# One core, cross attention and quantised FFN: the first stage's statistics, activation table and weight sums in another order

## The reference

```python
def _layernorm(x, axis=-1, eps=1e-05):
    m = jnp.mean(x, axis=axis, keepdims=True)
    v = jnp.var(x, axis=axis, keepdims=True)
    return (x - m) / jnp.sqrt(v + eps)

x = x + _L0_xattn_ref(_layernorm(x), ctx_768, Wq, bq, Wk, bk, Wv, bv, Wo, bo)
x = x + _L0_ffn_ref(_layernorm(x), W1, b1, W2, b2)          # weights to -1, 0, 1
x = x + _L1_xattn_ref(ctx_768, _layernorm(x), mask, ...)     # ctx_768 is normalised in it
x = x + _L1_ffn_ref(_layernorm(x), ...)                      # 8 experts, two for each token

# in _L0_xattn_ref
q = x @ Wq + bq; k = y @ Wk + bk; v = y @ Wv + bv
out = softmax(q k^T * scale) v;  return out @ Wo + bo
# in bitlinear of _L0_ffn_ref
w_scale = clip(mean(abs(W)), EPS)
Wq = clip(round(W / w_scale), -1, 1) * w_scale
```

## Time and profile before

| what | us |
|---|---|
| median of three executions | 954.39 |
| lowest, highest of them | 952.44, 960.53 |
| the profiled execution's own time | 951.19 |
| its span in the trace | 949.4 |
| PE busy in the span | 878.0 |
| DVE busy | 638.1 |
| ACT busy | 531.1 |
| POOL busy | 384.7 |

### The profile page before, as it was taken

The page is one execution under the profiler, slowest core; times in us unless marked ns, Lnnn a source line. Parts: engine busy times, 40 slices in busy tenths (PEclk is TensorE's granted clock), DMA queues, the critical chain, the costliest instruction groups (busy, mean ns, idle before and its releaser), DMA issues.

```text
span 949.4 us, 15088 instructions
## 1 busy us (share of the span) xinstructions
PE 878.0 (92%) x4301; PEld 612.3 (64%) x4302; DVE 638.1 (67%) x1282; ACT 531.1 (56%) x847; POOL 384.7 (41%) x319
## 2 busy tenths in 40 slices
PE   8987769889999999999999999999999999999991
PEld 4644445545555555555457887778888887888881
DVE  4899987765567467456388778846666666566666
ACT  2548875546665755765555434326666665666650
POOL 2134424526667647657505545502222222222210
PEclk9999999999999999999999999999999999999996
DMA  9400000008487587578565200078711298426305
GB/s 308 102 1 1 0 0 1 1 4 319 160 319 281 195 332 293 200 302 312 214 248 189 100 1 1 12 274 364 277 60 33 69 353 337 182 78 259 108 24 177
DMA packets 49908, 154.05 MB, mean 162 GB/s; under 512 B 6266, under 2 KB 24438, under 8 KB 44236
## 3 DMA queue, kind: packets, MB, share of 16 engines
q1 hardware_dynamic: 46124, 144.25, 40.3%
q0 software_dynamic: 3744, 9.31, 3.1%
HBM read 97.85 MB, written 56.62 MB: 163 GB/s over the span
## 4 chain that ended last, share of the span: by engine, by line
PE 63%; DVE 16%; DMA 6%; ACT 6%; issue 5%; POOL 2%; SPq 1%; DVEq 0%; ACTq 0%; POOLq 0%
PE banks L1032 12%; PE banks L1283 6%; PE banks L1285 6%; PE banks L1284 6%; DMA aux<-moe_x,small 4%; PE banks L1001 4%; PE banks L1024 3%; PE banks L1025 3%; PE banks L939 2%; PE banks L1320 1%; PE banks L1322 1%; PE banks L1321 1%; PE banks L988 1%; PE banks L1296 1%; PE banks L1046 1%
## 5 line engine op out<-in xcount | busy, mean ns | idle before, releaser
L1032 PE MATMUL banks<-wexp 128*65 128x512 f32 (+1 forms) x288 | 149.2, 599 | 2.8 <-ACT wexp L1590 2.8
L662 POOL TENSOR_TENSOR cv_hl<-wexp,cv_hl 128x1024 fp32r<-128x1024 f32 x45 | 108.5, 2418 | 53.7 <-ACT cv_hl L1567 53.1
L1283 PE MATMUL banks<-ring,x_hi 128*128 x312 | 127.4, 408 | 0.0
L1285 PE MATMUL banks<-ring,x_lo 128*128 x312 | 122.1, 391 | 0.0
L1284 PE MATMUL banks<-ring,x_hi 128*128 x312 | 122.1, 391 | 0.0
L1590 ACT ACTIVATE wexp<-banks 128x512 f32<-128x512 f32 x128 | 76.3, 598 | 75.3 <-PE banks L1025 74.8
L2065 DVE TENSOR_REDUCE small<-banks 128x1 bf16<-128x1101 f32 x64 | 83.6, 1307 | 38.0 <-PE banks L1001 38.0
L1726 ACT ACTIVATE banks<-wexp 128x1024 f32 x72 | 73.4, 1020 | 47.7 <-DVE aux L2446 47.7
L1704 ACT ACTIVATE aux<-banks 128x512 f32<-128x512 f32 x78 | 46.6, 597 | 63.0 <-PE banks L1285 46.9
L1024 PE MATMUL banks<-q_hi,k_hl 128*128 128x512 f32 x144 | 75.3, 523 | 1.7 <-ACT q_lo L1558 1.0
L734 POOL DMA_INDIRECT moe_y<-aux,small x20 | 20.6, 1030 | 115.8 <-DVE aux L2456 115.8
(11 more groups left out here) (365 smaller groups left out, 2188.9 us busy)
## 6 DMA issues: line engine op xcount, KB each, us to landing
wsplit<-cv_hl SPq DMA_DIRECT2D x45, 1024.0 KB, 7.9
ring<-wsplit SPq DMA_DIRECT2D x32, 1280.0 KB
wexp<-in_L_ffn_w SPq DMA_DIRECT2D x40, 512.0 KB, 5.8
wexp<-in_expert_biases SPq DMA_DIRECT2D x8, 1152.0 KB, 6.6
ring<-wsplit SPq DMA_DIRECT2D x4, 1024.0 KB, 8.7
wexp<-moe_y SPq DMA_DIRECT2D x7, 512.0 KB, 6.1
wexp<-in_L_ffn_sw SPq DMA_DIRECT2D x5, 512.0 KB, 8.8
x_sb<-in_x SPq DMA_DIRECT2D x4, 512.0 KB, 8.0
```

The lines of the kernel that those rows point to most:

```text
L662: g.tensor_tensor(sides(hl[:, PIECE:2 * PIECE]), raw, sides(hl[:, 0:PIECE]).bitcast(f32), ALU.subtract).then_inc(s['cv_lo'], 1)
L1032: mm(pb[5 + half][0:DA, :], vh[b][0:w, c, :], pT[q % 3][0:w, :], start=c == 0, stop=c == len(KTILES) - 1).then_inc(s['a_pv'], 1)
L1283: mm(o[:], x_hi[u][:, kc, :], hi, start=kc == 0 and not primed, stop=False, skip_group_check=primed)
L1285: last = mm(o[:], x_lo[u][:, kc, :], hi, start=False, stop=primed and kc == KC - 1, skip_group_check=primed)
```

## The change

- DVE takes the context's statistics first, while x loads. Then it handles tiles 0 to 3 by themselves: statistics, aggregates, epsilon (columns 0 to 4 of `root_a`), and later their `norm`. The statistics of the second and third part of x lie ahead of that `norm`; those of the fourth part, with aggregates and `norm` for the other 12 tiles and the context, lie behind `tokens0(0)`.
- ACT loads the table of the square root before its first copy, takes the root of columns 0 to 4 behind the second result and that of 4 to 18 behind the last.
- PE's first filler has 28 dummy matmuls for 20, the second 6 for 16, and PE no longer waits for ACT's last copy ahead of the second.
- `shifted(0)` is called ahead of `magnitudes` rather than between its two sums. The second sum (`magnitude2`) goes to `between[0]`; `ternary` goes from `between[0]` to `between[1]`, ahead of `masks`; `weights_sums` goes to PE's second list and the copy of its result to the head of ACT's second list.

The whole diff:

```diff
--- before.py
+++ after.py
@@ -774,7 +774,7 @@
                     mm(pb[7][:], ones_b[:], ones_b[:].unsqueeze(1).to_broadcast([P, 4, P]), start=True, stop=True)
 
             pe.wait_ge(s['warm'], 1)
-            warm(20)
+            warm(28)
             pe.wait_ge(s['const'], 2)
             pe.wait_ge(s['ld_l0'], NLD['ld_l0'])
             for w in (l0_wk, l0_wv):
@@ -800,7 +800,6 @@
                     mm(o[0:SK, b * D:(b + 1) * D], vT0[:, ec, b * SK:(b + 1) * SK], l0_wo[:, ec, :], start=ec == 0, stop=False)
                 last = mm(o[0:SK, b * D:(b + 1) * D], ones[0:1, 0:SK], bo0[0:1, :], start=False, stop=True)
             full(last)
-            pe.wait_ge(s['prep_free'], unit[0])
 
 
             def turn_ctx():
@@ -825,7 +824,7 @@
                 full(mm(bank()[:, 0:2], ones[:], wsum, start=True, stop=True))
                 NLD['prep_w'] = unit[0]
 
-            pieces = [[weights_sums, turn_ctx], [], [], []]
+            pieces = [[turn_ctx], [weights_sums], [], []]
 
 
             G = 4
@@ -851,7 +850,7 @@
                                   stop=u == G - 1 and kc == KC - 1)
                 last.then_inc(s['g_sc'], 1)
 
-            warm(16)
+            warm(6)
             turned0(0)
             warm(5)
             scores0(0)
@@ -1432,15 +1431,16 @@
                 last.then_inc(s['prep_free'], 1)
 
             act.wait_ge(s['const'], 2)
+            ready(ACT.Sqrt)
             for dst, bias in ((kT0, bk0), (vT0, bv0)):
                 o = filled()
                 for ec in range(KC):
                     last = a(dst[:, ec, :], o[:, ec * SKB:(ec + 1) * SKB], ACT.Identity, bias=bias[:, ec:ec + 1])
                 last.then_inc(s['prep_free'], 1)
+            root(0, 4)
             kept((flat(m0), lambda o: o[:, 0:KC * SKB]), (c0[0:1, :], lambda o: o[0:1, KC * SKB:(KC + 1) * SKB]))
-            ready(ACT.Sqrt)
             kept((flat(vv0[0:SK]), lambda o: o[0:SK, 0:B * D]))
-            root(0, T + B)
+            root(4, T + B)
 
             def keep_ctx():
                 o = filled()
@@ -1457,7 +1457,7 @@
                 act.wait_ge(s['w_times'], k + 1)
                 a(flat(q), flat(raw), ACT.Sign, bias=cols[:, 32:33]).then_inc(s['f_pre'], 1)
 
-            pieces = [[lambda: kept((wabs, lambda o: o[:, 0:2])), keep_ctx], [lambda: times(0, w1_raw), lambda: times(1, w2_raw), lambda: signs(0, w1_raw, w1T)],
+            pieces = [[keep_ctx], [lambda: kept((wabs, lambda o: o[:, 0:2])), lambda: times(0, w1_raw), lambda: times(1, w2_raw), lambda: signs(0, w1_raw, w1T)],
                       [lambda: signs(1, w2_raw, w2T)], [lambda: ready(ACT.Sqrt), lambda: root(0, TB), lambda: keep_context(0)]]
 
             def tokens0(it):
@@ -1791,25 +1791,31 @@
             link(v.tensor_scalar(eno_sh[:], eno[:], float(SHARED), None, ALU.is_equal))
             v.tensor_copy(hot_sh[:], eno_sh[0:96, 0:1]).then_inc(s['r_hot_sh'], 1)
 
-            for k, name in enumerate(('ld_x', 'ld_x1', 'ld_x2', 'ld_x3')):
+            def aggregate(t0, t1):
+
+                for t in range(t0, t1):
+                    last = v.bn_aggr(mv[:, t, :], stats[:, t, :])
+                link(last)
+
+            def raw_stats(k, name):
                 ve.wait_ge(s[name], 16)
                 for t in range(4 * k, 4 * k + 4):
                     last = v.bn_stats(stats[:, t, :], x_sb[:, t, :])
-            link(last)
-
-            def aggregate(t0, t1):
-
-                for t in range(t0, t1):
-                    last = v.bn_aggr(mv[:, t, :], stats[:, t, :])
-                link(last)
-
-            aggregate(0, T)
+                return last
+
+            def raw_variances(c0, c1):
+                v.tensor_scalar(root_a[:, c0:c1], mv[:, c0:c1, 1], LN_EPS, None, ALU.add).then_inc(s['root_in'], 1)
+
             ve.wait_ge(s['ld_l0'], NLD['ld_l0'])
             for b in range(B):
                 link(v.bn_stats(root_t[0:SK, 8 * b:8 * b + 6], ctx_sb[0:SK, b, :]))
                 link(v.bn_aggr(mv[0:SK, T + b, :], root_t[0:SK, 8 * b:8 * b + 6]))
-            v.tensor_scalar(root_a[:, 0:T + B], mv[:, :, 1], LN_EPS, None, ALU.add).then_inc(s['root_in'], 1)
-            norm(0, T + B, 0.0)
+            link(raw_stats(0, 'ld_x'))
+            aggregate(0, 4)
+            raw_variances(0, 4)
+            raw_stats(1, 'ld_x1')
+            raw_stats(2, 'ld_x2')
+            norm(0, 4, 0.0)
             flat = lambda ap: ap.rearrange("p a b -> p (a b)")
 
 
@@ -1858,7 +1864,9 @@
                 last.then_inc(s['ctx_n'], 1)
                 ve.wait_ge(s['ld_w12'], NLD['ld_w12'])
                 v.tensor_reduce(wsum[:, 0:1], w1_raw[:], AX.XY, ALU.add, apply_absolute_value=True)
-                shifted(0)
+
+            def magnitude2():
+
                 v.tensor_reduce(wsum[:, 1:2], w2_raw[:], AX.XY, ALU.add, apply_absolute_value=True).then_inc(s['w_abs'], 1)
 
             def ternary():
@@ -1899,7 +1907,7 @@
                 link(last)
 
             sums_of = [sums4, sums4, sums4, mx4]
-            between = [ternary, masks, lambda: variances(0, TB), lambda: None]
+            between = [magnitude2, lambda: (ternary(), masks()), lambda: variances(0, TB), lambda: None]
             def shifted(it):
 
                 ve.wait_ge(s['g_sc'], it + 1)
@@ -1908,7 +1916,12 @@
                 v.tensor_tensor(p0[:], sc, mx4.unsqueeze(2).to_broadcast([P, 4, SK]), ALU.subtract).then_inc(s['g_sh'], 1)
 
             tokens0(0)
+            link(raw_stats(3, 'ld_x3'))
+            aggregate(4, T)
+            raw_variances(4, T + B)
+            norm(4, T + B, 0.0)
             tokens0(1)
+            shifted(0)
             magnitudes()
             for it in range(T // 4):
                 ve.wait_ge(s['g_p'], it + 1)
```

More of the change, by code:

```diff
@@ L1792, in _ @@
             v.tensor_copy(hot_sh[:], eno_sh[0:96, 0:1]).then_inc(s['r_hot_sh'], 1)
-            for k, name in enumerate(('ld_x', 'ld_x1', 'ld_x2', 'ld_x3')):
-                ve.wait_ge(s[name], 16)
-                for t in range(4 * k, 4 * k + 4):
-                    last = v.bn_stats(stats[:, t, :], x_sb[:, t, :])
-            link(last)
             def aggregate(t0, t1):
@@ L1804, in aggregate @@
                 link(last)
-            aggregate(0, T)
+            def raw_stats(k, name):
+                ve.wait_ge(s[name], 16)
+                for t in range(4 * k, 4 * k + 4):
+                    last = v.bn_stats(stats[:, t, :], x_sb[:, t, :])
+                return last
+            def raw_variances(c0, c1):
+                v.tensor_scalar(root_a[:, c0:c1], mv[:, c0:c1, 1], LN_EPS, None, ALU.add).then_inc(s['root_in'], 1)
             ve.wait_ge(s['ld_l0'], NLD['ld_l0'])
```

## The result

The changed kernel takes 962.49 us in the median of 20 runs (955.64 to 971.74), the kernel before 954.82 (952.44 to 960.53, 20 runs). The ratio is **1.0072** with an interval of 1.0056 to 1.0088, so the change costs 6.9 us. The ratio leaves out the longest run of the changed kernel, over 1.5% above its shortest; the medians of all runs lie 7.7 apart. Forecast were +6.2 us, slower by 0.65%.

The account below looks back on a forecast made before the run. The prediction took PE's matmuls to bound most of the kernel, and a chain of waits among PE, ACT and DVE the first stage. It summed 4.57 + 1.6 = +6.2 onto 954.39, giving 960.6 us, range 952.4 to 964.5.

Parts of the forecast that it names:

- The front: Preparation before round 0: ACT's copy of round 0 starts at 21.55 where it was 24.10, -2.5 us.
- The collision: Round 2's four normalisations on DVE run into POOL's 2.35 us instruction and are blocked by the port lock: +2.3 us.
- The order on ACT: ACT's long passes wait for the later `w_inv` and hold the copy of round 3 queued behind them: +4.57 us.
- The clock: Round 3's scores: PE's clock falls to the lower level after standing 5.0 us, adding 1.6 us.
- the shift of round 3: ACT's copy of round 3 moves from 46.77 to 51.34, +4.57 us, with no slack behind to take it back.
- No collision: Round 2: DVE gets all its normalisations in because POOL starts later or yields; +3.9 with the clock, 958.3 us; chance 0.12.
- The clock holds: Round 3: PE keeps its full clock after the idle time; +4.6, 959.0 us; chance 0.15.
- The front gains nothing: Round 0 stays at 24.1, held by a root or later x; +6.5 with the clock, 960.9 us; chance 0.12.
- Faster: ACT's three passes do not hold round 3, so the front's -2.6 reaches the end: 951.8 us; chance 0.06.
- cancelled: Something behind the stage that the trace doesn't show waits anyway and takes back the loss: 954.4 us; chance 0.10.

Follow-up runs that it names:

- first profile: Profiled execution of the changed kernel from its first measurement, against the kernel before: span 964.2 us; that measurement's ratio 1.0072.
- second profile: Profiled execution of the same changed kernel, measured again with no edit: span 958.8 us; that measurement's ratio 1.0080.
- experiment 2: Changed kernel with POOL's three wo instructions started only after PE has transposed round 3; ratio 1.0050 against the kernel before.
- experiment 8: experiment 4 with 9 dummy matmuls rather than 5 ahead of the scores of round 1; ratio 0.9954 against the kernel before.
- experiment 5: Kernel before with only the weights' new order (shifted(0) first, second sum and ternary scales later), old front kept; ratio 1.0093 against the kernel before.
- experiment 1: Changed kernel with the weights' second sum, reduction and ternary scales put back as before, new front kept; ratio 0.9994 against the kernel before.
- experiment 3: Changed kernel with dummy matmuls in PE's waits: 17 before round 2's transposes, 26 for 5 before round 3's scores; ratio 1.0024 against the kernel before.
- experiment 4: Edits of experiment 1 and experiment 2 together: new front, weights' order as before, POOL later; ratio 0.9957 against the kernel before.
- Experiment 6: experiment 2 with ACT's long passes moved behind the copy of round 3, ternary scales still in round 1; ratio 0.9956 against the kernel before.
- experiment 7: Changed kernel measured once more without an edit, for its second profile; ratio 1.0080 against the kernel before.

## Why the prediction was right

**The front.** Forecast -2.5 at the copy of round 0, measured -3.9 and -2.8. The second root is one half of the mechanism only. In the first profile ACT waited 1.54 for DVE ahead of it and made it at 20.05, with the copy behind it at 20.20; but PE's transposes ended at 20.16 (19.12 + 1.04) only, so the two were nearly level. In the second profile the root was made at 20.82, and the copy then waited for PE:

```profile
20.19 1.04 PE L836 MATMUL banks<-ident,aux 128*128 128x128 f32 x8
...
21.27 0.60 ACT L1465 ACTIVATE aux<-banks 128x512 f32<-128x512 f32 x1 [0.23 <-PE banks L836]
```

So it was in experiments 2 and 8 (0.66 and 0.21). The sum had put the eight added dummies at nothing. In the second profile the 28 took 9.12, to 10.4, and PE began the keys at about 10.25, though the context was there at 9.56; before, the 20 had ended at 8.3 and PE began at 9.75. In the first profile the 28 took 7.55 and held nothing up.

The rest is in the loads and in DVE's own terms. The context lay ready at 9.62 in the profile of before and between 8.28 and 9.56 in the others, experiment 5 with the front of before among them (8.29); the first part of x was used from 10.41 in the first profile and 11.17 in the second, where the sum has 10.98. I had held this landing fixed, since no load was moved; it moves by itself from execution to execution. From there to the end of the second root DVE and ACT needed 9.85 in both, 0.7 less than the 10.57 of the sum.

**The collision.** Forecast +2.3, measured 3.55 and 2.03, and 2.1 in experiment 1. The place and the mechanism were right. The spread goes with how many of POOL's three instructions are still to come when DVE arrives: at 31.14 in the first profile and 31.52 in experiment 3 the first has just begun (4.92 and 4.89), at 32.21 in the second profile and 32.93 in experiment 1 only the last is left (3.40 and 3.50). A longer gain at the front was partly paid back here. One normalisation took 2503 ns beside a POOL instruction of 2.34, where 0.4 is its time alone; at half rate it would be 0.8. That agrees with the exclusive lock that the Trainium skill states (SBUF — State Buffer, "SBUF: two separate sides"). The collision's price at the end of the kernel is 2 to 3.5 us: 2.1 by the trace of experiment 1, 2.7 by the medians of experiments 1 and 4, 3.5 by their ratios.

**The order on ACT.** Forecast +4.57 at the copy of round 3, measured +3.68 in the second profile; of the 0.9 between them, the front was 0.5 better than forecast at DVE's copy of round 0 and the collision 0.3 cheaper. In the first profile it was +8.66, with the other term below. Experiment 6 settles it: the same late `w_inv`, without the copy queued behind the passes, and 9.0 us are gone. That sum holds the clock's fall too, which goes with the stand.

**The clock.** This is the term that was mis-sized. I forecast 1.6, from a factor of 1.66 on a group of four matmuls and with part of the work back at full speed. In the second profile DVE's copy of round 2 came 7.08 behind ACT's copy (57.53 - 50.45), before 4.40 (51.17 - 46.77): 2.68. The marks of before:

```profile
47.91 0.78 PE L845 MATMUL banks<-wexp,ones 1*128 1x308 f32 x2
...
50.46 0.60 PE L868 MATMUL banks<-ident,aux 128*77 128x128 f32 x4
```

From the start of the scores to the start of the transposes of the probabilities PE took 2.55 there, and 4.82 in the second profile (51.55 to 56.37): 2.27 more, a factor of 1.89, with all of it at the low clock. Another 0.45 lies between the start of these transposes and DVE's copy, a part that the sum left out. The factor of 1.66 was read too low: the group of the earlier trace rows starts at 67.65, and the granted clock was still 0.91 on the mean until 67.90 and 0.50 only from there. The Trainium skill's start-to-start times (TensorE: Matmul & The Clock Gate, "Wait — 56ns, not 53.3ns?"), nearly a factor of 2, agree with the 1.89. That the 2.7 worked out from them is so near to 2.68 is in part luck, since it was for the scores alone. Too large and too small nearly cancelled: 3.68 + 2.68 = 6.4 against the forecast 6.2.

**What I didn't name** is a stand of PE in round 2. My own sum gives it: PE's product with the values (L876) ended at 36.99 before, so at 34.0 with the -3.0, and the normalisations end at 36.35, 2.4 later. I took PE's clock there as given. In the first profile the stand was 3.74, the clock fell, and round 1's copy came 5.0 later than in the second (46.55 and 41.56). That is most of the 5.4 by which this profile is longer than the other. How often it falls there in the 20 runs was not seen, since only one execution of each measurement has a trace. Their mean granted clocks lie between 0.963 and 0.978, with a median between 0.975 and 0.976; the first profile has 0.973, the second 0.981, a value that none of the 20 reaches. So all of them had more low clock somewhere than the second profile, but the record doesn't show where. The sum also carried the shift of round 3 unchanged to the end, and left out what came up in the first FFN tiles (2.5 in the second profile). That the measured +6.9 lies so near to +6.2 is therefore in part luck; the place of the passes, the collision and the low clock behind the stand are the mechanism as described.

**The rivals.** No collision: experiment 2 is that case, +4.8 measured and +3.9 forecast, with the clock down. The clock holds: experiment 3, +2.3 measured where 4.6 was forecast; its normalisations took 4.89 as well, so the low clock costs 4.6 to 5.3 us in all (against 1.0072 and 1.0080), more than I gave it. The front gains nothing: it did gain, 3.9 and 2.8 at the copy of round 0. Faster, and cancelled: experiments 4 and 6 show that a gain of this stage reaches the end, so nothing absorbs it.

## What to carry to other kernels

When a step is moved behind another, look at the queue of the engine that waits for it, not only at the engine that does it: the second sum was hidden work on DVE, and the price arose on ACT, where three long passes that wait for it stand ahead of a copy of 0.6 us that the next round needs. Ask of every stage that gets earlier what it will now run beside; a POOL job that cost nothing took back 2.1 of a gain of 2.8 us, and one wait on a semaphore gave it back. A stand of PE of 4.5 to 4.9 us was paid twice here, once as time and once as low clock behind it; where the stand can't be removed, dummy matmuls in it are worth trying (5 us here).

## What the runs showed of the hardware

- The low clock lasted longer than in the earlier trace rows although PE was busy: 12 us with PE busy for 11.88 of them in the changed kernel's round 2, 9.5 us in its round 3 (8.45 busy), 10 us in experiment 4 (9.65 busy) and nearly 7 in round 3 of the second profile, against 3.2 before. The forecast's 1.6 had part of the scores, 2.72 of work, back at full speed.
- Shorter stands were followed by a fall in some executions only. One of 0.9 in round 1 stands in the profiles of experiments 1 and 4, and the clock fell in 4. One of 2.2 to 2.3 in round 2 (experiments 1 and 7) had no fall behind it, the one of 3.7 (the changed kernel's first profile) had. Behind 4.5 to 4.9 it fell in all four profiles that have such a stand (changed, 2, 5, 7), and in experiment 3, where it was filled, it didn't. Experiment 5 also had a low stretch behind a stand of 1.10 that ended at 8.29 (0.66 on the mean from 10 to 20); before, a stand of 1.46 at the same place had none.
- Single executions of one kernel scatter with their mean granted clock: of the kernel before, 949.84 us at 0.985 and 959.48 us at 0.973. The order is not strict: the changed kernel took 959.37 us at 0.977 and 960.48 us at 0.981. One profiled execution is then a poor base for a median, and so is the difference of two: here they differ by 14.8 or 9.4 in their spans, the medians by 7.7.
- The table load that was moved is at 0.81 in the changed kernel, where ACT has nothing to do. PE's L791 lost its 0.27 of waiting for ACT by that, but ACT then waited 1.54 for DVE ahead of the second root, and that root and PE's transposes ended within 0.1 of each other, so little of it could reach the copy of round 0.
- Not every DVE instruction was held by POOL: in experiment 5 the sum of magnitudes (L1860) took 2.27 at 33.71 beside POOL's L602 (33.76, 2.35), as long as it took alone before, while the normalisations beside the same instruction took 3.40 to 4.92 for 1.37.
